# Message pass of a graph network: three producers and consumers in another order on TensorE and VectorE

## The reference, cut to what matters

```python
edge_feat = _mlp(edge_attr, W_edge, ...)            # relu, then batch norm over all edges
message = jnp.concatenate([x[row], x[col], edge_feat], axis=1)
message = _mlp(message, W_msg, ...)                 # relu(message @ W + b), batch norm
agg = jax.ops.segment_sum(message, col, num_segments=N)
return agg + node_feat
```

## Time and profile before

| | |
|---|---|
| time, median of 3 runs | 11309.91 us (11304.01 to 11315.23) |
| profiled execution, its own time | 11304.11 us |
| its span in the profile | 11302.3 us |
| TensorE busy / VectorE busy / GpSimd busy | 57% / 41% / 58% of the span |
| message pass (first to last step) | 515.5 us to 3360.7 us of the span |
| granted TensorE clock in it | 0.50 |

### The profile page before, as it was taken

How to read it: one execution, slowest core, us unless ns; L and a number is a source line. 1 busy time by engine, 2 the same in 40 slices (tenths; PEclk the granted TensorE clock), 3 DMA queues, 4 the chain that set the end, 5 groups by cost and what they waited for, 6 DMA issues and landing times. The chain is left out here.

```text
span 11302.3 us, 137890 instructions
## 1 busy us (share of the span) xinstructions
PE 6476.3 (57%) x31155; PEld 5674.4 (50%) x31155; DVE 4578.9 (41%) x11750; ACT 3536.6 (31%) x7293; POOL 6608.7 (58%) x6483
## 2 busy tenths in 40 slices
PE   4866666666665555555556555555556555555555
PEld 2355555555554444444446444444446444444445
DVE  5744444444443333333333333333333333333334
ACT  2611111111113333333332333333332333333332
POOL 0166666666645666666663666666663666666663
PEclk8555555555555666666665666666665666666665
DMA  6111111111112111111111111111111111111111
GB/s 119 33 32 32 32 32 32 32 32 32 32 25 34 34 35 34 34 34 34 34 34 26 34 34 35 34 34 35 34 34 25 35 34 34 35 34 34 34 34 25
DMA packets 339638, 395.84 MB, mean 35 GB/s; under 512 B 225961, under 2 KB 233503, under 8 KB 337399
## 3 DMA queue, kind: packets, MB, share of 16 engines
q0 software_dynamic: 206976, 330.75, 15.2%
q1 hardware_dynamic: 132615, 64.61, 3.0%
HBM read 368.10 MB, written 26.82 MB: 35 GB/s over the span
## 5 line engine op out<-in xcount | busy, mean ns | idle before, releaser
L764 POOL DMA_INDIRECT rows<-table_a,idx x4851 | 4786.3, 987 | 2692.3 <-issue 1579.1
L1346 PE MATMUL ps<-ident,work 128*128 128x128 f32 x4872 | 1187.9, 419 | 2583.7 <-issue 2446.6
L764 POOL DMA_INDIRECT rows<-table_m,idx x1617 | 1764.9, 1091 | 1081.0 <-PE ps L1002 556.2
L1363 PE MATMUL ps<-rows,work 128*128 x9744 | 1777.3, 353 | 954.4 <-ACT work L1295 852.7
L1346 PEld LDWEIGHTS ps<-ident,work 128*128 128x128 f32 x4872 | 935.2, 220 | 2677.9 <-issue 2534.4
L1363 PEld LDWEIGHTS ps<-rows,work 128*128 128x128 f32 x9744 | 1645.8, 262 | 1151.5 <-issue 1149.3
L1302 ACT ACTIVATE work<-work,small 128x896 f32<-128x896 f32 x696 | 724.9, 1042 | 3609.0 <-issue 2234.7
L1239 DVE SCALAR_TENSOR_TENSOR work<-dstf,big,select 128x224 f32 x696 | 314.4, 452 | 3157.1 <-SPq L707 1710.4
L1228 DVE CUSTOM_DVE_ANT_0 work<-work,ps 128x896 f32<-128x896 f32 x696 | 757.0, 1088 | 1234.8 <-issue 944.0
L1354 PE MATMUL ps<-ident,work 128*128 128x128 f32 x4872 | 1120.7, 403 | 84.1 <-DVE work L1249 51.3
L1002 PE MATMUL ps<-work 128*97 128x32 f32 x3248 | 577.4, 350 | 896.8 <-DVE work L928 892.9
(11 more groups left out here) (252 smaller groups left out, 6314.9 us busy)
## 6 DMA issues: line engine op xcount, KB each, us to landing
rows<-table_a,idx POOLq DMA_INDIRECT x4851
rows<-table_m,idx POOLq DMA_INDIRECT x1617
big<-edge_parts SPq DMA_DIRECT2D x231, 45.5 KB
edge_parts<-big SPq DMA_DIRECT2D x6, 1617.0 KB, 7.6
work<-edge_parts SPq DMA_DIRECT2D x50, 192.0 KB
table_a<-work SPq DMA_DIRECT2D x3, 2474.5 KB, 22.6
b_dram<-big SPq DMA_DIRECT2D x3, 1176.0 KB, 8.1
big<-b_dram SPq DMA_DIRECT2D x3, 1176.0 KB, 18.3
```

The source lines that it names most:

```text
L764: pool.indirect_dma_start(rows[:, k % RING, j, 0:width], None, table, bass.IndirectOffsetOnAxis(ap=idx[:, k // CHUNK, at:at + 1], axis=0)) ...
L1346: last = pe.transpose(ps[:, 4 + j // 4, (j % 4) * P:(j % 4 + 1) * P], prob[:, par, j, :], ident[:])
L1363: last = pe.matmul(ps[:, 6 + par, 0:D + 1], probT[:, par, j, :], rows_of(at("slot", 3))[:, j, 0:D + 1], start=(j == 0), stop=(j == TPG - 1))
```

## The change

On TensorE the three parts come in the order edge_product(q), message_product(q-1), node_sums(q-2). On VectorE `match` is cut in two: `match_turned` (turned match, then the window's rows) comes first, then add_source(q-1), add_squares(q-2), accumulate(q-2), and last `match` (plain match and count). The pace of the gathers is told by `u_ready` (edge_product) where it was `s_ready` (node_sums), with a lead of -1 where it was 2: gather(g) waits until u_ready has reached g+1, so until edge_product(g) is done; before, until node_sums(g-3) was done. No instruction is added or removed.

```diff
-LEAD_M = 2
+LEAD_M = -1
...
-                        if not (isinstance(g, int) and g <= emit.lead):
+                        if not (isinstance(g, int) and g <= max(emit.lead, 0)):
                             pool.wait_ge(emit.steps_told, g - emit.lead)
...
-            steps_told, lead = step_sems["s_ready"], LEAD_M
+            steps_told, lead = step_sems["u_ready"], LEAD_M
...
+                def match_turned(q, par, at):
+                    dve.wait_ge(s["dst_ready"], q + 1)
+                    if not (isinstance(q, int) and q < 2):
+                        dve.wait_ge(s["pre_ready"], 2 * q - 2)
+                    # eqT (tensor_scalar), then: wait win_ready q; b_low; wait low_ready q + 1; b_win
...
+                def match(q, par, at):
+                    # eq (scalar_tensor_tensor); wait eq_ready q + 1; inside (tensor_reduce)
...
                 def step(q, par, live, at):
+                    if live(0):
+                        match_turned(q, par, at)
+                    if live(1):
+                        add_source(q - 1, (par - 1) % 2, at)
+                    if live(2):
+                        add_squares(q - 2, (par - 2) % 2, at)
                     if live(2):
                         accumulate(q - 2, (par - 2) % 2, at)
                     if live(0):
                         match(q, par, at)
-                    if live(2):
-                        add_squares(q - 2, (par - 2) % 2, at)
-                    if live(1):
-                        add_source(q - 1, (par - 1) % 2, at)
...
                 def step(q, par, live, at):
+                    if live(0):
+                        edge_product(q, par, at)
+                    if live(1):
+                        message_product(q - 1, (par - 1) % 2, at)
                     if live(2):
                         node_sums(q - 2, (par - 2) % 2, at)
-                    if live(1):
-                        message_product(q - 1, (par - 1) % 2, at)
-                    if live(0):
-                        edge_product(q, par, at)
```

More of the change, by code:

```diff
@@ L904, in match @@
                                       ALU.subtract, ALU.is_equal).then_inc(s["eqt_ready"], 1)
-                    dve.wait_ge(s["eq_ready"], q + 1)
-                    dve.tensor_reduce(inside[:, par], eq[:, par], AX.X, ALU.add).then_inc(s["inside_ready"], 1)
+                    if not (isinstance(q, int) and q == 0):
+                        dve.wait_ge(s["win_ready"], q)
+                    dve.tensor_scalar(b_low, b_all[:, bass.ds(at("parts", 0) + ROW_B, D)],
+                                      selects[0:3 * WA, bass.ds(at("table", 0) + WA + 1, 1)], None, ALU.mult).then_inc(s["low_ready"], 1)
                     dve.wait_ge(s["low_ready"], q + 1)
@@ L910, in match @@
                                              ALU.mult, ALU.add).then_inc(s["win_ready"], 1)
+                def match(q, par, at):
+                    d = dstf[:, bass.ds(at("ready", 0), TPG)]
+                    dve.scalar_tensor_tensor(eq[:, par], d.unsqueeze(2).broadcast_to([P, TPG, WA]), base_w[:, bass.ds(at("window", 0), 1)],
+                                             iota[:, bass.ds(at("shift", 0), WA)].unsqueeze(1).broadcast_to([P, TPG, WA]),
+                                             ALU.subtract, ALU.is_equal).then_inc(s["eq_ready"], 1)
+                    dve.wait_ge(s["eq_ready"], q + 1)
+                    dve.tensor_reduce(inside[:, par], eq[:, par], AX.X, ALU.add).then_inc(s["inside_ready"], 1)
                 def add_source(k, par, at):
```

## The result

The changed kernel takes **10,945.0 us** (median of 4 runs, 10,944.1 to 10,949.7) against 11,310.9 us (11,304.0 to 11,315.2), a ratio of 0.9678 with a 95% interval of 0.9661 to 0.9695. It is 366 us faster, where I forecast 583: the direction was right, the time is 218 us over my 10,727 and 65 us over the range.

A forecast was written before the change was run, and what follows sets the result against it. Before, TensorE and VectorE taking turns bounds the 12.26 us step; after, GpSimd's gathers at 9.75 us. Saving 228 x (12.25 - 9.75) = 570 plus 13 at the ends, 583 us, gives 10,727 us; range 10,560 to 10,880.

The forecast's parts named there:

- The ring is cut: Message pass: TensorE and VectorE stop taking turns, so none of TensorE's 3.88 us idle beside its 8.38 us need remain.
- GpSimd's price, 9.75 us a step: Message pass: seven gather issues bound each step, 8.75 us unstretched, chosen as 9.75 between 9.64 and 9.88.
- Does anything hold GpSimd back?: Step on gather(g) waiting for edge_product(g): the gather could start 3.7 us before GpSimd is free, so no wait.
- The stretching of issues: Issues starting during VectorE's L901, L886 or L928 run longer: 0.47 + 0.21 + 0.21 = 0.89 us a gather by formula.
- less stretched: Rival: L901 and L928 fall between issues, a step is 8.75 to 9.3 us, time 10,500 to 10,625 us; chance 0.17.
- my own formula, 11,297 - 228 x (12.25 - T): Whole-kernel time in us for a message-pass step of T us, with 13 us at the ends taken off.
- VectorE and its register load: Message pass: 3.3 us of load per pair falls before the turned match, 6.7 us a step; double buffers absorb lateness.
- The pace ring: Rival: edge product, gather, landing and message close over two steps, 22.4 us, so 11.2 us a step, 11,060 us; chance 0.04.
- waits for L977 in most steps: Sign in the profile after: GpSimd showing these waits would mean the forecast is wrong and the pace ring closes.
- TensorE bounds: Rival: TensorE's register load isn't hidden, at least 10.03 us a step, up to 10.6, time 10,790 to 10,920 us; chance 0.12.
- the slower case: Rival: the pace ring closes over a single step, 22.4 us a step, 13,600 us; chance 0.02.
- no effect: Rival: the two engines still take turns through some unseen wait, 12.2 us a step; chance 0.02.

The follow-up runs named there:

- i0_after: The changed kernel, unchanged, run in the quick condition: 9,300.2 us, 9.18 us a step, beside 10,014.2 us for the kernel before.
- e3_old_order_u0: The kernel before with only the gathers' pace moved to u_ready, lead 0, quick condition: 10,008.7 us beside 10,009.4 us for the kernel before.
- m1_lead2: The changed kernel with its lead put back from -1 to 2, slow condition: 10,951.0 us beside 11,303.5 us for the kernel before.
- f2_after: The changed kernel, unchanged, run again in the slow condition: 10,890.4 us, 10.61 us a step, beside 11,275.6 us for the kernel before.
- f3_before: The kernel before, unchanged, run again for its profile in the slow condition: 11,269.3 us beside 11,275.6 us for the kernel before.
- l2_old_order_u0: The kernel before with only the gathers' pace moved to u_ready, lead 0, slow condition: 11,292.2 us beside 11,306.1 us for the kernel before.

## Why the prediction was off

- **The ring is cut.** Right. Both waits of the earlier trace rows are gone, and without gathers the same order runs at 8.32 us a step with TensorE full. My 8.38 stands.
- **GpSimd's price, 9.75 us a step: this term failed, and with it the step "Does anything hold GpSimd back?", which put its waits at nothing.** I built the term from issues, 8.75 us without stretching and about 1 us of it, while the turned matches came 10.73 us apart on average over the pass (231 intervals from 504.0 to 2982.1): 228 x (10.73 - 9.75) = 223 us too little, where the time was missed by 218. (The ends nearly cancel: gather(3) starts at 528.98, 13 us before my 542, and the pass ends 20 us after the last issue, where I had 13.) What the sum left out is GpSimd's idle time beyond the 0.30 us gaps: 2300 - 1501.57 - 1498 x 0.30 = 349 us in 214 steps, 1.6 us a step. I had let a telling of edge_product wake GpSimd 0.87 us after the product's end, with 3.7 us to spare; in the timeline above 5.4 us pass (2017.23 to 2022.62).
- **The stretching of issues** was too large, so the two parts of the 9.75 were off in opposite ways. An issue takes 1002 ns, 57 over its 945, 0.4 us a group where it was (1091 - 945) x 7 = 1.0, so the rival "less stretched" had the issue time right. What I had misread is L901: in the changed kernel 203 issues start inside the same instruction, now L893, over 0.25 us before its end, and none takes 0.97 us or more. The stretched ones stand beside L931 (108 of 116) and L886 (97 of 98) and end 0.82 us after them, as in these two rows:

```profile
2032.54 0.85 DVE L886 TENSOR_TENSOR work<-work 128x672 f32<-128x672 f32 x1
2032.60 1.61 POOL L764 DMA_INDIRECT rows<-table_m,idx  x1 [1.18 <-issue]
```

  Without the 0.47 us that my formula gave to L901 it has 0.42, and 0.40 was measured; what stretched the issue beside L901 before isn't shown. (The Trainium skill, page "SBUF — State Buffer", section "Who interferes with whom", infers that `tensor_tensor` does not stop descriptor writing; this trace does not agree: L886 is a `tensor_tensor`, and the issue that starts inside it takes 1.61 us.) The quick run, at 9.18 us a step, pays 7 x (1.004 + 0.30) = 9.13 and little else: there the sum by issues holds, and my 9.75 was too much. In the slow condition the two errors partly offset each other.

- **The trace before held a nearer price.** Its attention stage issues seven gathers a group too, and in the quick condition GpSimd never pauses in it, so that there gathers set its pace. In the kernel before, slow, 4000 to 4900 us, inside one layer:

```profile
4000.00:4900.00 900.00, 465.52 (x2352) 431.63 (x2352) 342.25 (x1013) 338.12 (x757) 583.57 (x592) 0.63 0.18 34
```

  That is 900 x 7 / 592 = **10.64 us a group**, with GpSimd busy 65%, where issuing asks for about 8.8 (attention in the quick i0_after, 1500 x 7 / 1195 = 8.79). The earlier trace rows already had 2000 x 7 / 1268 = 11.0 for a stretch with a break between layers in it. And the timeline of the kernel before shows how it comes about:

```profile
5011.00 0.94 POOL L764 DMA_INDIRECT rows<-table_a,idx  x1 [0.30 <-issue]
5015.49 1.46 POOL L764 DMA_INDIRECT rows<-table_a,idx  x1 [3.55 <-issue]
...
5036.86 1.38 POOL L764 DMA_INDIRECT rows<-table_a,idx  x1 [3.65 <-remote]
```

  From 5015.49 on come 14 issues with gaps of 0.30 us, then 3.65 us of nothing. Of 351 runs of issues in this trace's attention (a run ends at a gap of over 0.5 us) 334 have just 14; in e3_old_order_u0, quick, the 1617 issues of a layer are one run. In the changed kernel the same figure appears in the message pass, 14 issues from 2001.55 and the next at 2022.62: 21.07 us for two groups, 10.5 each. In three traces of the slow condition message pass and attention agree: 10.75 and 10.64 us in the pair's changed kernel, 10.81 and 10.64 in m1_lead2, 10.61 and 900 x 7 / 593 = 10.62 in f2_after, whose attention is this row:

```profile
4000.00:4900.00 900.00, 468.67 (x2376) 433.37 (x2374) 342.41 (x1015) 340.07 (x761) 593.48 (x593) 0.64 0.17 34
```

  With 10.64 in place of 9.75 my own formula, 11,297 - 228 x (12.25 - T), gives 10,930 us, 15 us from the result. That was found with the result known, and why two stages with different waits should share a period isn't shown.
- **VectorE and its register load.** As forecast: the load lies ahead of the turned match (374.7 us over 95 heads of pairs, 3.9 us each) and the double buffers absorb it, since TensorE is full without gathers.
- **The pace ring.** As I priced it (11.2 us a step by its own length) it isn't what closes: with a lead of 2, three steps more, the time is the same in either condition (10,951 and 9,283 us). My sign for it, waits for L977 in most steps, can't be read cleanly: in the slow trace GpSimd's waits for L982, which is that line now, are named 21 times, and 99 more are unnamed, in 214 steps. **TensorE bounds** was wrong for the change as it is, and is right as soon as gathers take under 8.3 us a step. Neither the slower case nor that of no effect came about.
- **The clock** stayed at 0.50 in the pass, before, after and with TensorE full.
- **What is shown and what is open.** Shown in the slow condition: the loss of some 550 us against an order without gathers needs GpSimd's indirect issues (10,358 without any, 10,393 with plain transfers of the same bytes), and five of them in a step of 8.3 us don't bring it. Not shown is why. One idea is a cap, no more than seven issues in 10.65 us (theory 5); the other that issues without a pause hold TensorE's tellings until GpSimd itself, for want of a telling, runs dry (theory 1). Two rows of the kernel before speak against a hard cap: this is the first issue of an attention layer, and the one after the first 28.

```profile
3470.30 0.96 POOL L764 DMA_INDIRECT rows<-table_a,idx  x1 [46.89 <-DMA idx<-in_src_dram]
...
3510.63 0.94 POOL L764 DMA_INDIRECT rows<-table_a,idx  x1 [4.72 <-remote]
```

  Those 28 end at 3505.91 with gaps of 0.30 us alone: four groups in 35.6 us, 8.9 each, in the slow condition. The late tellings with five gathers speak against the cap as the whole story too. For it speaks that the average stays at 10.61 to 10.68 us in the attention of every slow trace, also where the runs are of another length (f3_before has 254 of 14 and 140 of 7). Six in a step of the slow condition would have helped to part the two. Why the conditions differ isn't known either. The starts of TensorE's next matmul, on time in the rows above, and the semaphores' own records, late, agree that it is the telling that comes late and not the matmul.

## What to carry to other kernels

Before you price a unit as "so many instructions by so many nanoseconds", look in the same trace for a stage in which that unit's same work comes as fast as it can, and take its period from there: the pauses that no instruction record shows are in it. Here one row of attention gave 10.64 us where the sum of issues gave 8.8 and then 9.75. It is a check of a price, and no proof: in the quick condition the sum of issues was right. And the same kernel took 13% longer at one time than at another, so run the kernel before beside every experiment, and compare only what ran together.

## What I had not expected of the hardware

- Two conditions: the kernel before took 11,276 to 11,311 us in one and 10,006 to 10,014 us in the other. The message pass doesn't tell them apart (12.26 us a step in the kernel before, slow, and in e3_old_order_u0, quick). Nearly all of it lies in attention, three layers of 231 groups at 10.64 against 8.79 us: 693 x 1.85 = 1,280 us.
- In the slow condition GpSimd mostly makes 14 indirect issues and then stands still, 3.56 us in the median in the attention of the kernel before, and other engines' tellings mostly come through in that pause. Runs of 28 at the head of each layer, and of 7, occur as well.
- In the slow condition records of TensorE's tellings are missing even where no one waited long: of the 233 of s_ready in l2_old_order_u0 the trace holds 27, of the same kernel in the quick condition (e3_old_order_u0) all 233. In the kernel before 64 of u_ready's are there, and ScalarE starts 0.12 us after the edge products in 226 of 232 steps. So a missing record is not a late telling; it was a sign of the slow condition that I had in hand.
- TensorE's order alone brought 267 us and VectorE's alone 102 us in the slow condition. That the two add up to about the 352 to 385 us of the whole change there is chance, as far as the runs show: each half is limited by a ring, and the whole by gathers and pauses (in the quick condition the whole brought 714 us).
